# A mixture-of-experts tile's output rows are stored from SP's queue instead of GpSimd's

## The reference, cut to what matters

```python
xf = x.reshape(-1, h)                       # 4096 tokens of 128 features
scores = sigmoid(xf @ gate_w + bias)        # 8 experts
top_scores, top_idx = jax.lax.top_k(scores, 2)
top_scores = top_scores / (sum(top_scores) + 1e-06)
w = zeros((T, E)).at[arange(T)[:, None], top_idx].add(top_scores)
up = einsum('th,ehi->tei', xf, up_w) + up_b
hact = gelu(up)
eo = einsum('tei,eih->teh', hact, down_w) + down_b
combined = einsum('teh,te->th', eo * 0.1, w)
shared = (gelu(xf @ sw_up + sb_up) @ sw_down + sb_down) * 0.1
out = shared + combined                     # then divided by the row's largest |value|
```

## Time and profile before

| | |
|---|---|
| median of 3 runs | 692.84 us (689.39 to 694.08) |
| the profiled execution's own time | 686.2 us |
| its span | 684.6 us, mean granted TensorE clock 0.984 |
| busy: TensorE, ScalarE, VectorE, GpSimd | 641.7, 479.7, 433.8, 394.3 us |
| 39 stores of rows on GpSimd (line 2082) | 21.6 us of issuing, 555 ns each |
| 64 scatters, 64 gathers on GpSimd | 63.5 and 64.3 us |
| SP's DMA queue | 52.62 MB, 24.5% of the 16 DMA engines' time |
| GpSimd's DMA queue | 13.07 MB, 5.9% |

### The profile page before, as it was taken

The page is one execution under the profiler, slowest core; times in us unless marked ns, Lnnn a source line. Parts: engine busy times, 40 slices in busy tenths (PEclk is TensorE's granted clock), DMA queues, the critical chain, the costliest instruction groups (busy, mean ns, idle before and its releaser), DMA issues.

```text
span 684.6 us, 11622 instructions
## 1 busy us (share of the span) xinstructions
PE 641.7 (94%) x3699; PEld 437.7 (64%) x3699; DVE 433.8 (63%) x999; ACT 479.7 (70%) x763; POOL 394.3 (58%) x558
## 2 busy tenths in 40 slices
PE   7998999999998989999998999998989999999994
PEld 5565556655555646479887999976565664555642
DVE  3675676687879788653633644203668788777762
ACT  4866797887988777586443555643989887978563
POOL 5436377578878887813442455255677677725353
PEclk9998999999999999999999999999999999999998
DMA  9067750000000000068775587710111111000003
GB/s 247 4 237 281 261 215 9 21 11 19 18 21 15 26 26 20 28 197 266 250 250 181 178 250 246 215 43 27 34 31 30 31 28 28 12 0 16 16 1 93
DMA packets 46183, 66.45 MB, mean 97 GB/s; under 512 B 6753, under 2 KB 29114, under 8 KB 46122
## 3 DMA queue, kind: packets, MB, share of 16 engines
q1 hardware_dynamic: 39856, 52.62, 24.5%
q0 software_dynamic: 6208, 13.07, 5.9%
q10 hardware_dynamic: 58, 0.02, 0.0%
HBM read 37.31 MB, written 27.85 MB: 95 GB/s over the span
## 4 chain that ended last, share of the span: by engine, by line
PE 34%; POOL 10%; issue 9%; DVE 5%; DMA 4%; ACT 2%; POOLq 1%; SPq 1%; DVEq 0%; ACTq 0%
PE PS L1183 7%; POOL got L2097 4%; PE PS L1259 3%; PE PS L1163 2%; DMA got<-expert_rows,IU 2%; POOL H L2028 2%; PE PS L975 2%; PE PS L981 1%; PE PS L987 1%; PE PS L1170 1%; POOL xl L2034 1%; POOL expert_rows L2069 1%; PE PS L1171 1%; PE PS L1172 1%; PE PS L1083 1%
## 5 line engine op out<-in xcount | busy, mean ns | idle before, releaser
L1923 ACT ACTIVATE GF<-PS,XN 128x256 f32<-128x256 f32 (+1 forms) x156 | 68.3, 455 | 59.4 <-PE PS L1163 28.3
L2069 POOL DMA_INDIRECT expert_rows<-five,IU x64 | 63.5, 992 | 42.0 <-DMA expert_rows<-five,IU 21.0
L2097 POOL DMA_INDIRECT got<-expert_rows,IU x64 | 64.3, 1004 | 39.0 <-DMA got<-expert_rows,IU 21.7
L1183 PE MATMUL PS<-WE,GF 128*128 128x128 f32 x568 | 83.6, 277 | 1.4 <-ACT GF L1923 1.4
L1401 DVE TENSOR_REDUCE MX<-PS 128x4 f32<-128x896 f32 (+2 forms) x96 | 61.3, 685 | 27.3 <-PE PS L1046 27.0
L1183 PEld LDWEIGHTS PS<-WE,GF 128*128 128x128 f32 x568 | 75.5, 193 | 3.1 <-ACT GF L1923 2.0
L1884 ACT ACTIVATE PA<-PS 128x1024 f32<-128x1024 f32 x64 | 64.9, 1039 | 10.4 <-PE PS L1067 10.1
L2058 POOL TENSOR_SCALAR_AFFINE_SELECT PA<-PA 128x256 f32<-128x256 f32 x128 | 50.9, 427 | 13.6 <-ACT PA L1884 13.5
L2028 POOL TENSOR_SCALAR H<-xc,MOD 128x256 f32<-128x256 f32 x56 | 32.5, 588 | 39.0 <-DVE xc L1366 38.5
L2082 POOL DMA_DIRECT2D expert_rows<-YT x39 | 21.6, 555 | 54.4 <-issue 34.2
L1163 PE MATMUL PS<-XS,WE 128*128 128x256 f32 (+1 forms) x192 | 47.1, 357 | 4.6 <-DVE XS L1648 4.6
(11 more groups left out here) (337 smaller groups left out, 1748.2 us busy)
## 6 DMA issues: line engine op xcount, KB each, us to landing
WE<-in_experts SPq DMA_DIRECT2D x39, 512.0 KB
expert_rows<-five SPq DMA_DIRECT2D x16, 1024.0 KB, 9.0
XT<-expert_rows SPq DMA_DIRECT2D x32, 128.0 KB
expert_rows<-YT POOLq DMA_DIRECT2D x32, 128.0 KB
BD<-in_L_ffn_down_b SPq DMA_DIRECT2D x39, 64.0 KB
PA<-in_L_attn_x SPq DMA_DIRECT2D x8, 256.0 KB, 5.2
out<-yo SPq DMA_DIRECT2D x8, 256.0 KB, 2.4
expert_rows<-five,IU POOLq DMA_INDIRECT x64
```

What stands on the lines that cost most here:

```text
L1183: m = pe.matmul(bk[:, b], g[:, b], wd[:, k, :], start=(k == 0 and t == 0), stop=(k == 3 and t == blocks - 1))
L1923: act.activation(GF[slot["gf", kind, u, k]][:, 0:n], bank("up", kind, u, k)[:, 0:n], ACT.Gelu, bias=bias).then_inc(sems["gelu"], 1)
L2069: pool.indirect_dma_start(out=XD[:, :], out_offset=bass.IndirectOffsetOnAxis(ap=IU[:, c, n, k:k + 1], axis=0), in_=HT[c % 2][:, k, :], in_ ...
L2097: pool.indirect_dma_start(out=got[b][n][:, k, :], out_offset=None, in_=XD[:, :], in_offset=bass.IndirectOffsetOnAxis(ap=IU[:, c, n, k:k + ...
```

## The change

The function `store_rows` moves, word for word, from GpSimd's program to SP's. The list of steps is unchanged, so on SP each store stands where the list has it: between the fetches and, for tile 0, ahead of `load_late`. Its DMA now runs in SP's DMA queue. Semaphores, buffers and sizes are as before.

```diff
@@ def gpsimd(pool)
-        def store_rows(t):
-            w.wait_ge(*at("ev", "t", t))
-            n = rows(t)
-            row = pool.value_load(EI[0:1, 1, t:t + 1], min_val=0, max_val=E * CAP)
-            pool.dma_start(XD[bass.ds(row, n), :].rearrange("(p k) d -> p (k d)", k=n // 128), YT[t % 3][:, 0:n]
-                           ).then_inc(rows_out[t % 3], 16)
-
...
-        do = {"ln_mod": ln_mod, "xlo": xlo_, "pjl": pjl, "kzp": kzp, "causal": causal, "scatter": scatter, "wsl": wsl, "store_rows": store_rows, "gather": gather,
+        do = {"ln_mod": ln_mod, "xlo": xlo_, "pjl": pjl, "kzp": kzp, "causal": causal, "scatter": scatter, "wsl": wsl, "gather": gather,
@@ def sync(sp)
+        def store_rows(t):
+            w.wait_ge(*at("ev", "t", t))
+            n = rows(t)
+            row = sp.value_load(EI[0:1, 1, t:t + 1], min_val=0, max_val=E * CAP)
+            sp.dma_start(XD[bass.ds(row, n), :].rearrange("(p k) d -> p (k d)", k=n // 128), YT[t % 3][:, 0:n]
+                           ).then_inc(rows_out[t % 3], 16)
+
...
-        do = {"rowin": rowin, "load_late": load_late, "fetch": fetch, "store": store}
+        do = {"rowin": rowin, "load_late": load_late, "fetch": fetch, "store_rows": store_rows, "store": store}
```

## The result

| | before | changed |
|---|---|---|
| median of four runs each | 691.12 us (687.27 to 694.08) | 700.51 us (698.31 to 702.24) |
| ratio of changed to before | | 1.0153, 95% interval 1.0102 to 1.0203 |
| profiled execution, own time (span) | 686.2 (684.6) us | 699.1 (697.3) us |
| issue of XT 38 | 438.82 | 454.11 |
| start of fetch 0 to issue of XT 38 | 146.5 us | 162.8 us |

Slower by 1.5%, about 10 us; the prediction was 706 in 697 to 717, slower by over 1% at 0.83. The kernel before now has a fourth run, which moves its median from 692.84 to 691.12. The medians are 9.4 us apart, the two profiled executions 12.9, and the forecast was 13.6 on top of 692.84. So of the 5.9 us between 706.4 and 700.5, 1.7 are the base, 0.7 the size of the change in the profiled executions, and 3.5 that the medians lie closer together than those two executions.

The account below looks back on a forecast made before the run. The prediction took SP's queue, full from tile 4 to 38, as the bound. XT 38 issued 14.0 us later, -0.4 for its landing and 0 for the last store gave +13.6 on 692.84: 706 us, range 697 to 717.

Parts of the forecast that it names:

- The bound: Expert stage: SP's queue is full from tile 4 to 38, wanting 4.0 us a tile against 3.43 for a full tile.
- What a store and a fetch cost: On SP a store takes 1.08 us, a fetch 2.9; 30 fetches and 29 stores after store 4 take 118.3 us.
- The sum: Whole kernel: 14.0 us at XT 38's issue, -0.4 for landing, 0 for the last store, together +13.6 us.
- The start: Tiles 6 and 7: store 0 ahead of load_late delays fetches, so TensorE is 5.7 us late at XT 7.
- The event behind the scatters: Near 360 us, late GpSimd stores make VectorE and TensorE wait; 6.3 us go, but ahead of where SP takes over.
- TensorE at -0.6 us, the lead used up near tile 25: Full tiles: start delay 5.7 less 6.3 us; SP loses over 0.5 us a tile, then each tile waits for its fetch.
- The terms behind XT 38: Stage end: landing of XT 38 takes 3.7 us instead of 4.07, -0.4; last store's 3.0 us unchanged, 0.
- the delay goes to the end whole: Behind the last `xt`: shared-expert work and gathers start from the last tile, so the remaining 241.7 us stay.
- The signs: Trace marks: SP's `ev` waits under 8 us, XT 7's `xt` waits 2 to 3, VectorE's 7.0 gone, last `xt` near 456.
- The queue has room: Rival: the 6.3 us on GpSimd go, SP's 24.8 us of waits and lead absorb the stores; 686.5 us, chance 0.06.
- Slower by much more: Rival: stores among 0.5 MB loads stretch issues and free YT's buffers later; 716 us and more, chance 0.13.
- Little changes: Rival: on SP fetches shrink to 2.69 us and landings to 2.8; 698 us or a few less, chance 0.15.

Follow-up runs that it names:

- cost_alone: Kernel before, stores left on GpSimd; at the moved stores' places SP waits, loads the row and issues a one-row 512-byte DMA to scratch. Ratio 1.0372.
- row_kept: Changed kernel, but each store uses the row number its fetch had loaded, with no table load of its own. Ratio to before 0.9959.
- bias_in_we: Changed kernel, but the expert's bias comes as 128 more columns of the weights' tile, so two DMAs a fetch. Ratio to before 0.9995.
- steady_sp: Kernel before with only stores 17 to 38 moved to SP, stores 0 to 16 left on GpSimd. Ratio to before 1.0106.
- first_sp: Kernel before with only stores 0 to 16 moved to SP, stores 17 to 38 left on GpSimd. Ratio to before 1.0020.
- five_sp: Kernel before with only stores 9 to 13 moved to SP, with their own table loads. Ratio to before 0.9900.
- lean_sp: Changed kernel with row numbers kept from the fetch, bias inside the weights' tile, and store 0 behind load_late and fetch 6. Ratio to before 0.9832.
- kept_late0: Changed kernel with row numbers kept from the fetch and store 0 behind load_late and fetch 6; three DMAs a fetch. Ratio to before 0.9905.

## Why the prediction was right

**The bound.** SP's queue full from tile 4 to 38: so it was, by its waits (0.3 us in all from 335 to 455 us), by cost_alone, which fills the queue without the stores' data, and by row_kept and bias_in_we, which shorten it and keep the data.

**What a store and a fetch cost.** Expected 1.08 and 2.9 us, measured 1.12 and 2.90 in the mean; the issue was 0.356 instead of 0.333 in the median, the table load 0.266. The chain of 30 fetches and 29 stores was put at 118.3 us, from 334.9; it took 119.9, from 334.5. XT 38 was expected at 452.9 and came at 454.11. With the measured 1.13 for a store, steady_sp was foretold to within 0.6 us; first_sp came out 1 to 3 us below what was expected.

**The sum, and luck in it.** The profiled execution of the changed kernel began fetch 0 1.0 us earlier than that of the kernel before. Counted from fetch 0, XT 38 is 16.3 us later, not 14.0. Behind it the changed kernel is 2.6 us shorter, not 0.4. The two misses cancel, 13.7 against 13.6, and that they do is luck. The ratio of the timed runs makes 10.5 us, 7 to 14 with its interval, so 13.6 lies at its upper end.

**The start.** Expected: `xt` 6 waits 3.1 us and `xt` 7 2.6, together 5.7. Measured 5.3 at tile 7, but as one wait of 4.20 at tile 6 and then matmuls at a low clock: the granted clock is 0.64 from 329 to 333 us, and the two groups of lines 1163 and 1183 from 329.37 us on took 1.06 and 1.84 us, where before they took 0.60 and 1.05. XT 7 still sets the time of `xt` 7, as expected: by the chain it landed at 329.95 + 3.21 = 333.16, for an `xt` at 333.21. TensorE, at the low clock, took until then to get there, so no wait shows. I had named "2 to 3 us at XT 7" as the mark, and no such wait is seen.

```profile
329.95 3.21 DMA XT<-expert_rows
```

**The event behind the scatters.** Taken as 6.3 us and hidden: gone between tiles 7 and 16 (from 5.3 late to 0.7 early, 6.0 us), and worth 7.0 by itself in five_sp.

**The step that failed** is "TensorE at -0.6 us, the lead used up near tile 25". The -0.6 was right at tile 16. But fetch 17 stands behind stores 11 to 13, and VectorE's cast of tile 17's weights then waits 2.47 us for its data. By the chain the delay goes on through VectorE's work to TensorE's first matmuls with tile 17's weights at 382.19, and TensorE loses 3 us there, at a place that I had not looked at. The chain, then the casts:

```profile
372.17 3.38 DMA XT<-expert_rows
375.57 0.43 DVE WH L1659
...
380.15 1.20 DVE WLO L1380 x2
...
382.19 0.39 PE PS L1170
```

```profile
375.57 0.43 DVE L1659 CAST WH<-WE 128x512 fp32r<-128x512 f32 x1 [2.47 <-DMA XT<-expert_rows]
...
413.17 0.43 DVE L1659 CAST WH<-WE 128x512 fp32r<-128x512 f32 x1
417.64 0.43 DVE L1659 CAST WH<-WE 128x512 fp32r<-128x512 f32 x1 [1.04 <-DMA XT<-expert_rows]
```

The second row of the casts is tile 27's, which still comes without a wait, the third is tile 28's: the lead lasted three tiles longer than I had it; that this is because TensorE was itself late is argued. Neither moves the end, which SP's chain sets.

**The terms behind XT 38, mis-sized.** Landing and what follows were put at -0.4 and 0. Measured: the last `xt` comes 457.61 - 454.11 = 3.5 us behind the issue, where before it was 4.1: -0.6. But it isn't a landing that TensorE waited for: its matmuls of tile 37 at the low clock lasted until then, which I had only in the high end, as "1 more". The tile itself took 0.2 us more. From `ev` 38's end (462.18) to the store's landing (464.43) it is 2.3 us instead of 3.0, -0.7, since the landing took 1.53 us, less than either end of my bounds. And it is another 1.4 us less from there to the end of the kernel, of which no run here shows the cause; but it comes again wherever the last stores are SP's. 15.3 - 0.6 + 0.2 - 0.7 - 1.4 = 12.8, and the spans differ by 12.7. The step that failed here is that the delay goes to the end whole: what lies behind the last `xt` was to stay at 241.7 us and was 239.7.

**The signs.** SP's waits for `ev` were to fall below 8 us; up to 460 us they are 8.3, 5.1 of them store 0's. The wait of 7.0 us is gone, though one of 2.4 is left. The last `xt` came at 457.61, not near 456, and without a wait. Of the signs of being wrong none came.

**The rivals.** "The queue has room" was wrong as a whole, but names the gain that five_sp takes. "Slower by much more" didn't come: VectorE's waits for stores fell, fetches stayed at 2.9 us. "Little changes" needed fetches of 2.69. The rule by which initiating DMAs on several engines saves only the sequencer's time, "usually small relative to the DMA itself" (the Trainium skill, "DMA: Bandwidth & Descriptors", Issuing engines are not separate DMA queues), is half right here. lean_sp has the stretch of five_sp, so in which queue 34 of the stores ran made a difference of about 1 us at most. But a store's 1.12 us on the sequencer stand beside 2.5 us to its landing, and on a full queue they were most of the loss.

## What to carry to other kernels

Before moving a DMA to an engine "that only issues DMAs", add up its queue: number of steps times their full cost on the sequencer (table loads and checks, not the issue alone) against the time a tile leaves it; here 2.9 + 1.1 against 3.43 us. Take the mean of a step and not its floor, and leave room: kept_late0 was planned at 3.3 us and ran at 3.46, and its queue was full. Look at what the moved instruction stands ahead of, not only behind: one wait in front of eleven unrelated loads cost 6 us. And if a move helps at one place, move it at that place: five stores of 39 gave 1.0%, all 39 cost 1.5%, until their cost on the queue was cut. Last, look behind the stretch too: with the last stores on SP, what follows XT 38 was 2.3 to 5.1 us shorter than in the kernel before.

## What the runs showed of the hardware that was not expected

- Behind a DMA of a single 512-byte row on SP, the next table load took 482 ns in the median, against 268 to 271 ns for the same load, a fetch's first, in the twelve other kernels; the cause stays open.
- A store of 128 KB issued from SP amid 0.5 MB loads in the same queue landed after 2.5 us in the median in the changed kernel, after 4.4 in row_kept and 3.5 in lean_sp; GpSimd's landed after 4.2 in five_sp. The last store, 64 KB with nothing behind it, took 1.53 us from SP and 1.80 from GpSimd. Over all kernels the medians are 2.0 to 4.4 us from SP and 3.5 to 4.3 from GpSimd: they overlap, and no run isolates what sets them.
- The stretch ahead of the experts varies from execution to execution by up to 6 us (fetch 0's start), with a granted clock between 40 and 100 us of 0.94 in the kernel before and 0.86 to 1.00 in the others. A difference between two single executions has to be taken over the stretch that an edit touches.

The stores among the DMA issues, KB each and median us to landing, for the second point: changed kernel, row_kept, lean_sp, and GpSimd's in five_sp.

```profile
expert_rows<-YT SPq DMA_DIRECT2D x32, 128.0 KB, 2.5
```

```profile
expert_rows<-YT SPq DMA_DIRECT2D x32, 128.0 KB, 4.4
```

```profile
expert_rows<-YT SPq DMA_DIRECT2D x32, 128.0 KB, 3.5
```

```profile
expert_rows<-YT POOLq DMA_DIRECT2D x27, 128.0 KB, 4.2
```
